# Causal self attention: query tiles of the maxima in reversed order within a head

## What is computed

```python
h = _ln(x, ln1_g, ln1_b)
qkv = _lin(h, attn_qkv_w, attn_qkv_b)
q, k, v = jnp.split(qkv, 3, axis=-1)
a = _attend(_heads(q), _heads(k), _heads(v), causal=True)   # 16 heads of 16
x = x + _lin(a, attn_proj_w, attn_proj_b)
```

## Times and profile before

| | |
|---|---|
| median of three runs | 3936.55 us |
| lowest and highest | 3933.16 and 3937.19 us |
| profiled execution | 3936.01 us |
| its span, first to last instruction | 3934.2 us |
| mean granted TensorE clock | 0.955 |
| instructions | 68606 |

### The profile page before, as it was taken

One profiled execution on the slowest core, in us unless ns is written; L12 is line 12 of the kernel. 1 busy time (PEld: TensorE's weight loads), 2 busy tenths in 40 slices (PEclk: granted clock), 3 DMA queues, 4 the chain that ended last, 5 costly groups with the idle time before them and its releaser, 6 DMA issues. The chain is left out here.

```text
span 3934.2 us, 68606 instructions
## 1 busy us (share of the span) xinstructions
PE 3657.2 (93%) x21586; PEld 2042.0 (52%) x21586; DVE 2777.7 (71%) x6843; ACT 2459.2 (63%) x5254; POOL 1989.8 (51%) x1987
## 2 busy tenths in 40 slices
PE   6999999997996999999999999998799999999998
PEld 3444444443882344433333334443687777777776
DVE  4666677774665777788999978774766666666664
ACT  2555567775331677778888877776325666666665
POOL 3555533322322323358888843231445677776765
PEclk7999999998996999989999899999899999999999
DMA  4433353431002434333222244431100000000000
GB/s 106 100 85 82 80 113 84 86 84 48 1 1 49 116 88 89 78 67 86 62 63 63 60 99 89 89 83 49 45 1 12 12 7 12 13 7 12 12 1 12
DMA packets 135373, 220.51 MB, mean 56 GB/s; under 512 B 42720, under 2 KB 44640, under 8 KB 133216
## 3 DMA queue, kind: packets, MB, share of 16 engines
q1 hardware_dynamic: 135008, 216.02, 23.7%
HBM read 59.69 MB, written 5.51 MB: 17 GB/s over the span
## 5 line engine op out<-in xcount | busy, mean ns | idle before, releaser
L1105 ACT ACTIVATE prob<-ST 128x512 f32<-128x512 f32 (+3 forms) x2304 | 1151.3, 567 | 440.0 <-PE ST L647 435.9
L1343 DVE TENSOR_REDUCE mx<-MX 128x1 f32<-128x512 f32 x1536 | 964.2, 683 | 221.7 <-PE MX L647 220.2
L647 PE MATMUL MX<-stk 48*128 48x512 f32 (+3 forms) x2560 | 897.5, 441 | 59.2 <-DVE mx L1336 14.3
L647 PE MATMUL ST<-stk 50*128 50x512 f32 (+3 forms) x2560 | 917.8, 444 | 2.6 <-ACT prob L1105 1.8
L647 PEld LDWEIGHTS MX<-stk 48*128 48x128 f32 x2560 | 420.6, 191 | 707.1 <-DVE mx L1343 293.6
L1788 POOL TENSOR_SCALAR prob<-prob,mx 128x128 f32<-128x128 f32 (+3 forms) x512 | 558.5, 1104 | 274.1 <-DVE mx L1523 274.1
L647 PE MATMUL OUT<-prob,V 128*32 128x512 f32 (+3 forms) x5120 | 664.4, 592 | 8.0 <-POOL prob L1730 4.1
L647 PEld LDWEIGHTS ST<-stk 50*128 50x128 f32 x2560 | 424.3, 189 | 51.1 <-ACT prob L1105 23.8
L1336 DVE CUSTOM_DVE_ANT_0 MX<-MX,W_even 128x512 f32<-128x512 f32 x512 | 348.0, 701 | 39.3 <-PE MX L647 38.7
L1723 POOL TENSOR_TENSOR prob<-prob,W_odd 128x512 f32<-128x512 f32 x256 | 324.8, 1283 | 90.7 <-ACT prob L1105 90.3
L1340 DVE CUSTOM_DVE_ANT_0 MX<-MX,later 128x128 f32<-128x128 f32 (+3 forms) x512 | 238.0, 519 | 124.8 <-PE MX L647 124.0
(11 more groups left out here) (190 smaller groups left out, 7254.8 us busy)
## 6 DMA issues: line engine op xcount, KB each, us to landing
stk<-hi SPq DMA_DIRECT2D x640, 128.0 KB, 3.8
stk<-lo SPq DMA_DIRECT2D x320, 128.0 KB, 3.9
misc<-misc SPq DMA_DIRECT2D x160, 128.0 KB, 2.6
sums<-spread SPq DMA_DIRECT2D x80, 256.0 KB
misc<-in_ctx_t SPq DMA_DIRECT2D x24, 512.0 KB, 6.8
W_even<-in_w SPq DMA_DIRECT2D x2, 2048.0 KB, 10.1
XH<-in_ctx_rows SPq DMA_DIRECT2D x8, 512.0 KB, 3.5
X<-in_x_t SPq DMA_DIRECT2D x1, 3584.0 KB, 14.0
```

The costliest lines, as they stand in the source:

```text
L647: return nc.tensor.matmul(o, l, r, start=start, stop=stop)
L1105: nc.scalar.activation(prob_at(k)[:, q0:S], STB[k % RING][:, q0:S], ACT.Copy if addmask else ACT.Exp).then_inc(ex_done, 2 if addmask else 1)
L1343: nc.vector.tensor_reduce(m, bank[:, :], AX.X, ALU.max).then_inc(mx_red, 1)
```

## The change

In causal attention the query tiles of a head are taken from the last to the first: a function `query_tile` turns k into qt, and both `max_tile` functions use it. TensorE multiplies another slice of queries with another width of keys at place k; VectorE reduces that width and writes the maximum into the column `at` where it stood before, so that all that reads `mx` finds the same numbers in the same places. The score tiles, the other stages, all semaphores and their counts, the banks and the runs stay.

```diff
+        def query_tile(causal, k):
+
+            return NT - 1 - k % NT if causal else k % NT
...
                 def max_tile(causal, U, half, k):
 
-                    i, qt = divmod(k, NT)
+                    i, qt = k // NT, query_tile(causal, k)
                     wait(pe, mx_red, TILES * (U if k >= RING else U - 1) + before(k) + 1)
...
                 def max_tile(sm, U, half, k):
                     _, causal, addmask = ATTN[sm]
-                    qt = k % NT
+                    qt = query_tile(causal, k)
+                    at = k // NT * NT + qt
                     waits(dve, (mx_full, TILES * U + k + 1), apart=addmask or causal)
-                    bank, m = MXB[k % RING], mx[:, half, k:k + 1]
+                    bank, m = MXB[k % RING], mx[:, half, at:at + 1]
```

## The result

The changed kernel takes **3940.4 us** (median of 20 runs, 3927.6 to 3953.6), the kernel before, in 20 runs, 3925.0 us (3911.1 to 3937.2). The ratio is **1.0039, 95% interval 1.0026 to 1.0053**: slower by some 15 us, and the interval excludes 1. The three runs of before that the prediction was made against, 3933 to 3937 us, were at the upper end of its own spread. So the predicted 3940.0 us met the measured median by luck: the starting point, 3936.55, was 11.5 us too high, and the change, +3.4 where about +15 was measured, 12 us too small.

What follows compares the result with a forecast made beforehand. TensorE, busy 93% of the span, was taken as the bound, with reduction waits the only change: 1.0 + 2.4 + 0 = +3.4 us on 3936.0 gives 3939.4, median 3940.0; range 3932.0 to 3947.0.

Steps and rivals of the forecast that it cites:

- nothing but waits changes: First stage, causal self attention: same tiles issued and reduced, busy times stay, the sum consists of waits alone: +3.4 us.
- The first slot: Slot u = -1, max tiles alone: K and Q jobs wait longer for reductions; +1.0 us, bounds 0.5 and 1.3.
- Even slots: Eight slots, u = 0, 2 to 14: Q slips behind later reductions, 0.3 us each, +2.4 us, bounds 0.8 to 3.6.
- Tile 16 is no help or harm: Even slots: this tile waits until 244.54 in either order, supposedly for the stk<-lo transfer issued at 241.02.
- Odd slots: Seven slots, u = 1 to 13: gain at the start given back before the first product; sum 0, bounds -2.1 to +2.1 us.
- the hole that the wide first tile leaves: Start of odd slots: the wide opening tile arrives 0.18 us later; +0.1 us put for the hole before the first product.
- equal waits fell or didn't: Argument on output projections in even slots: low clock follows equal waits by chance, so four falls may become two.
- rival A: Output projections in seven even slots: GpSimd wait grows to 1.3 us, low clock follows all; +4.5, total 3944.5 us; chance 0.22.
- B: Turn of the slots: odd slots keep 0.53 + 0.18 us, even slots lose nothing; -4.0, 3932.6 us; chance 0.13.
- C: Even slots: their loss lies under the transfer holding tile 16 and the score queue; +1.0 alone, 3937.5 us; chance 0.15.
- The gain at the turn of the slots: Start of odd slots: last two tiles reduced 0.53 us sooner, so the wait of tile 1 behind tile 0 goes.

Runs made afterwards that it cites:

- experiment 2: Idle matmuls in odd slots and ahead of even slots' GpSimd wait (changed order 1.0109, old order 1.0066), then only the latter (1.0054, 1.0011), against the kernel before.
- experiment 3: Order reversed for heads 4 and 7 alone, against the kernel before: ratio 1.0005 (0.9984 to 1.0027).

## Why the prediction was right and wrong

**Right: nothing but waits changes, and what the waits cost.** VectorE's, ScalarE's and GpSimd's busy times stay within 8 us of the whole span. At full clock the change costs 3.7 to 4.0 us (with 0.8 or with 1.1 for the first slot, below), forecast 3.4.

**The first slot, forecast +1.0:** 30.79 us against 29.98 in the profiled pair, +0.8, both mostly at low clock. At full clock, from the kernels of experiment 2, whose first slot has no idle matmul in it, changed order and then old order:

```profile
40.16:67.30 27.14, 24.81 (x64) 13.04 (x64) 17.83 (x74) 1.96 (x3) 9.14 (x10) 1.00 0.39 63
```

```profile
39.52:65.54 26.02, 24.28 (x64) 12.94 (x65) 17.39 (x73) 1.96 (x3) 9.14 (x10) 1.00 0.39 64
```

+1.12. Both ends lie inside the bounds of 0.5 and 1.3.

**Even slots, forecast +0.3 each:** the place was right and so was the size there. Q comes about 0.3 us later behind tile 12, and TensorE waits 0.28 us for a reduction. But the slot keeps only about 0.2 of it: for one thing run 3 is shorter (tile 11 to tile 12: 1.99 us where it was 2.16), which the sum had not counted. "Tile 16 is no help or harm" was wrong in part: that tile took the wait, in u = 6 it was held longer by its transfer than by the reduction (0.49 us, Q 0.43 later), and u = 2, counted among the eight, gave nothing because such a transfer held it in both kernels.

**Odd slots, forecast 0 (bounds -0.3 to +0.3): the term that was mis-sized,** +0.22 each on the mean. The step is "So the gain is given back before the first product; I put +0.1 for the hole that the wide first tile leaves." The backlog of 2560 columns is indeed equal, but the hole is 0.34 (VectorE idle for 0.52 instead of 0.18), and in the slot shown the product came 0.44 later. The same cause, a wide tile that opens a burst late, had been priced at 0.18 from the earlier trace rows; here it comes on top of reductions that are done sooner, since the two tiles before it became cheap: both lengthen the hole.

**Wrong: "Against it: equal waits fell or didn't, so chance may as well turn four into two."** With it the sum put the clock at nothing. The clock was given to rival A, with +4.5 us and a chance of 0.22, and without it the kernel would not have been slower by more than 0.2%, the outcome with a chance of 0.20. A's place was right and too narrow. Its condition was met or nearly so: in the profiles after six and seven of seven waits for GpSimd were followed by the low clock, in those of before four and three. The price per wait was about right. But the reason it gave, a wait grown to 1.3 us, was not there, and it looked at that one place. The falls behind run 2, 7 of 15 slots in both profiles after and 2 in both before, were in no case of the prediction. Worse, the waits of the sum were priced at full clock and by themselves: in the profiles 2.4 us more of idle time in twelve slots went with some 16 us more of busy time, in the timed runs the clock cost at least as much again as the waits.

The prediction leaned on the Trainium skill ("TensorE: Matmul & The Clock Gate", Part 1, What's actually happening): the watching of activity runs free of the kernel, and the turning point differs from run to run. I drew from it that the order could not shift the number of falls. The runs show that this doesn't follow: the places of the falls differ between two profiles of one kernel, as the Trainium skill has it, but their number goes with the order of the work (clock 0.98 and 0.98 against 0.92 and 0.93 over the twelve slots).

**Rivals B and C.** The gain at the turn of the slots is real at its place (tile 1 stands 0.31 us behind tile 0 instead of 0.56) and lost again in the hole ahead of the wide tile; the kernel that takes it alone (experiment 3) shows no gain. C's even slots of unchanged length were not found.

**What stays open.** That the reversed order gets less clock is shown by two profiles against two, by the kernel with only the later slots reversed and by the clocks of the timed runs. How much of the 15 us that makes is known only as half or more. Which waits set it off is not known: filling the one before the output projection left the timed ratio of the orders at 1.0043 but took most of the falls out of the one profile, and idle matmuls for the odd slots could not be placed without a wait of their own. Nor is it settled whether the two halves add up or need each other. No version tried beats the kernel before.

## What to carry to other kernels

Where TensorE is the bound and the granted clock is already below 1 in places, a wait has two prices: its own length, and what a longer stretch at the lower clock costs behind it. Here the second was one to three times the first in the timed runs and more in the profiles, so a sum of waits taken at full clock came out too small. Reversing an order so that the last jobs of a burst are cheap also makes its first ones dear; look at what the consumer does in between (it idled for the wide tile) and not only at equal sums. An execution that happens to be profiled can be one of the slowest: hold its clock against those of the timed ones before its lengths are taken for the kernel's. And three runs of a kernel whose executions spread by 26 us don't fix its time to 0.2%: the same kernel had a median 11 us lower in 20.

## What the runs showed of the hardware

- The same work in two odd slots, behind nearly the same engine activity, ran once largely at 1.2 GHz and once at 2.4: behind 2.16 busy us of 2.40 the eight matmuls took 1.94 us, behind 2.13 of 2.37 they took 1.07.
- Waits of 1.12 to 1.13 us were followed by the lower clock in four and three of seven cases before and in six and seven of seven after, although the waits have the same length. With most of the wait filled (0.20 to 0.23 us idle) it was still four of seven.
- Low clock is nowhere to be seen in TensorE's idle time: it shows as busy time (301.1 to 318.1 us for the same 1968 matmuls), so the share of 93% on the page of the profile stays 93%.
- The first slot took 30.8 us at a mean clock of 0.58 and 27.1 at 1.00, in the same order: the clock at which a stage is entered is worth more than the change in that slot (0.8 to 1.1).
- Over 82 executions of one kernel the mean granted clock ran from 0.950 to 0.970 and the time from 3905 to 3960 us, about 23 us per 0.01.
